# Attention stage: batch loops written out and interleaved, powers of the successor matrix made in the first loop

## The reference

```python
Xq = (H @ W_lin.T).reshape(bt, n, h, dh)
Xv = (H @ W_val.T).reshape(bt, n, h, dh)
e = einsum('behd,hd->beh', leaky_relu(Xq[:, src] + Xq[:, dst], 0.2), a) + log(A0[src, dst] + EPS)
m = segment_max(e_t, src)            # per source node, over its edges
ex = exp(e_t - m[src]); attn = ex / segment_sum(ex, src)[src]
Y = segment_sum(attn * Xv[dst], src)
return Y @ W_out.T
```

## Time and profile before

| | us |
|---|---|
| median of 3 runs | 6786.41 (6783.37 to 6788.06) |
| the profiled execution's own time | 6792.14 |
| its span, first to last instruction | 6790.4 |
| TensorE busy | 5355.4 (79%) |
| VectorE busy | 4564.6 (67%) |
| ScalarE busy | 2311.9 (34%) |
| mean granted TensorE clock | 0.93 of full |

### The profile page before, as it was taken

One profiled execution on the slowest core, in us unless ns is written; L12 is line 12 of the kernel. 1 busy time (PEld: TensorE's weight loads), 2 busy tenths in 40 slices (PEclk: granted clock), 3 DMA queues, 4 the chain that ended last, 5 costly groups with the idle time before them and its releaser, 6 DMA issues. The chain is left out here.

```text
span 6790.4 us, 109815 instructions
## 1 busy us (share of the span) xinstructions
PE 5355.4 (79%) x33047; PEld 3803.4 (56%) x33047; DVE 4564.6 (67%) x27007; ACT 2311.9 (34%) x7369; POOL 93.6 (1%) x128
## 2 busy tenths in 40 slices
PE   4666788888877769969899976993546699776999
PEld 4555566666666534446566653662333477554676
DVE  7888888888888853379999997775562333424333
ACT  1222222222222235449599881110110233201333
POOL 0000000000000000000000000000000000000000
PEclk9999999999999999969999987996778799876999
DMA  1000000000000000010000000000000000000000
GB/s 46 2 2 2 2 3 5 3 4 4 4 4 3 4 21 13 7 54 6 6 4 6 4 3 8 1 1 0 25 28 0 13 0 0 9 0 13 0 0 25
DMA packets 27823, 56.57 MB, mean 8 GB/s; under 512 B 6186, under 2 KB 16835, under 8 KB 25539
## 3 DMA queue, kind: packets, MB, share of 16 engines
q1 hardware_dynamic: 27330, 50.79, 2.2%
HBM read 38.20 MB, written 12.58 MB: 7 GB/s over the span
## 5 line engine op out<-in xcount | busy, mean ns | idle before, releaser
L2007 DVE SCALAR_TENSOR_TENSOR f_ACC<-f_yp,f_CG,f_ACC 128x128 f32<-128x128 f32 x1024 | 288.4, 344 | 461.6 <-DVEq L2005 461.6
L1952 PEld LDWEIGHTS f_yp<-f_W,f_hs 128*128 128x128 f32 x4096 | 490.0, 192 | 92.6 <-issue 91.8
L1886 PE MATMUL f_hp<-f_rows,f_W 128*128 128x512 f32 x1024 | 531.5, 602 | 5.1 <-ACT U L1896 3.0
L1054 ACT ACTIVATE e_XD<-e_X,e_scal 128x60 f32<-128x60 f32 x2048 | 527.5, 333 | 17.5 <-DVEq L918 15.7
L710 PE MATMUL h_small<-h_part,ones 128*128 128x2 f32 x1024 | 300.6, 363 | 294.3 <-DVE h_jd L579 198.4
L1983 ACT ACTIVATE f_hs<-f_hp,f_b 128x512 f32<-128x512 f32 x512 | 347.7, 685 | 539.7 <-ACTq L1982 539.7
L655 ACT ACTIVATE h_VW<-h_v,h_s 128x8 f32<-128x8 f32 (+3 forms) x512 | 154.8, 302 | 1082.6 <-DVE h_s L417 1082.6
L1942 PE MATMUL f_hp<-f_XT,f_W 128*128 x1024 | 484.4, 601 | 33.0 <-PEq L2236 33.0
L703 PEld LDWEIGHTS h_ax<-h_XM,h_parts 128*128 128x128 bf16 x11520 | 480.8, 114 | 40.9 <-issue 40.9
L1952 PE MATMUL f_yp<-f_W,f_hs 128*128 128x128 f32 x4096 | 493.5, 275 | 0.0
L710 PEld LDWEIGHTS h_small<-h_part,ones 128*128 128x128 f32 x1024 | 256.6, 311 | 415.0 <-DVE h_jd L579 287.6
(11 more groups left out here) (716 smaller groups left out, 11363.2 us busy)
## 6 DMA issues: line engine op xcount, KB each, us to landing
f_S<-in_f_W SPq DMA_DIRECT2D x64, 128.0 KB, 2.3
X<-in_x SPq DMA_DIRECT2D x1, 4096.0 KB, 16.3
held<-g0e_HL SPq DMA_DIRECT2D x16, 256.0 KB, 2.0
g_HL<-held SPq DMA_DIRECT2D x16, 256.0 KB, 2.8
f_W<-in_f_W SPq DMA_DIRECT2D x2, 2048.0 KB
spill<-f_xts SPq DMA_DIRECT2D x16, 256.0 KB, 2.0
f_rows<-spill SPq DMA_DIRECT2D x16, 256.0 KB, 2.7
f_W<-in_f_W SPq DMA_DIRECT2D x4, 1024.0 KB
```

The lines of the kernel that those rows point to most:

```text
L1054: ins = nc.scalar.activation(XD[b][:, k, h, :], X[:, :], ACT.Identity, bias=scal[b][:, k, 2 * h:2 * h + 1])
L1886: nc.tensor.matmul(self.hp[s % 3][:, :], self.W1[:, e, j * P:(j + 1) * P], self.rows[:, g % 2, :], start=True, stop=True).then_inc(self.h_ ...
L1952: ins = nc.tensor.matmul(yp[:, u % 2, k, :], hs[:, u % 2, c, k * P:(k + 1) * P], W2[:, u * UC + c, :], start=(c == 0), stop=(c == UC - 1))
L2007: ins = V_.scalar_tensor_tensor(ACC[:, k, :], yp[:, u % 2, k, :], CG[:, k * E + e:k * E + e + 1], ACC[:, k, :], ALU.mult, ALU.add)
```

## The change

Both loops are written out (no `Fori`, semaphores count up to 16 and are waited for by their value). TensorE's order in turn t of the first loop becomes: PGa of batch t, PL and PV of batch t - 1, then in turns 1, 3, ..., 13 one squaring of the successor matrix (PN and PNT), then PS of batch t - 2. VectorE normalizes batch t + 1 at the head of turn t. PL, PS and PV have one PSUM bank each instead of two; the freed banks hold PN and PNT. `NT` keeps all eight powers (8 instead of 2 halves), ScalarE copies PN to `NX`, VectorE PNT to `NT`. A max round is then PM and one maximum, written in place to `MM`; `MN` is gone. The last sum has its own PSUM tile. In the second loop TensorE makes PY of batch t, then PO of batch t - 1, and VectorE weights batch g + 2 before it adds batch g. Eleven semaphores are new, three are gone.

The diff, cut to its core:

```diff
-        NX, NT = sb("NX", [P, 2, EB, NE]), sb("NT", [P, 2, EB, NE])
+        NX, NT = sb("NX", [P, 2, EB, NE]), sb("NT", [P, 8, EB, NE])
...
+            def round_at(turn):
+                return turn // 2 if turn % 2 == 1 and turn // 2 < ROUNDS - 1 else None
...
                 def _(dve):
+                    def rows(g):
+                        if g >= 2:
+                            dve.wait_ge(g_made, g - 1)
+                        normalize(nc, dve, ch, done, XG[:, g % 2], X, mean, rstd, g * GT, GT).then_inc(xg_full, 1)
+                    rows(0)
+                    for turn in range(B + 2):
+                        if turn + 1 < B:
+                            rows(turn + 1)
+                        if 1 <= turn <= B:
+                            g = turn - 1
+                            dve.wait_ge(v_made, g + 1)
+                            V_.tensor_copy(VT[:, :, g, :], PV[:, 0:EB * D].rearrange("p (e d) -> p e d", e=EB)).then_inc(vt_full, 1)
+                            dve.wait_ge(lx_full, g + 1)
...
+                            V_.scalar_tensor_tensor(LR[:, g % 2, :], LX[:, g % 2, :], 0.2, LX[:, g % 2, :], ALU.mult, ALU.max).then_inc(l_full, 1)
+                        if round_at(turn) is not None:
+                            r = round_at(turn)
+                            dve.wait_ge(jump_made, r + 1)
+                            V_.tensor_copy(NT[:, r + 1, :, :], PNT[:, :, :]).then_inc(nt_full, 1)
+                        if turn >= 2:
+                            g = turn - 2
+                            dve.wait_ge(s_made, g + 1)
...
                 def _(pe):
-                    with pe.Fori(0, B // 2) as i:
+                    for turn in range(B + 2):
+                        if turn < B:
+                            pe.wait_ge(xg_full, turn + 1)
+                            if turn >= 2:
+                                pe.wait_ge(g_full, turn - 1)
...
+                        if 1 <= turn <= B:
+                            g = turn - 1
+                            pe.wait_ge(g_full, g + 1)
+                            if g >= 1:
+                                pe.wait_ge(lx_full, g)
+                            nc.tensor.matmul(PL[:, 0:NE], linT[:, :], GS[:, g % 2, 0:NE], start=True, stop=True).then_inc(l_made, 1)
+                            if g >= 1:
+                                pe.wait_ge(vt_full, g)
...
+                        if round_at(turn) is not None:
+                            r = round_at(turn)
+                            if r > 0:
+                                pe.wait_ge(nx_full, r)
+                                pe.wait_ge(nt_full, r)
...
+                        if turn >= 2:
+                            g = turn - 2
+                            pe.wait_ge(l_full, g + 1)
+                            if g >= 1:
+                                pe.wait_ge(ee_full, EB * g)
...
                 def _(act):
+                        if round_at(turn) is not None:
+                            r = round_at(turn)
+                            act.wait_ge(jump_made, r + 1)
+                            nc.scalar.copy(NX[:, (r + 1) % 2, :, :], PN[:, :, :]).then_inc(nx_full, 1)
...
                     for r in range(ROUNDS):
+                        pe.wait_ge(max_in, r + 1)
                         for e in range(EB):
                             for f in range(EB):
+                                ins = nc.tensor.matmul(PM[:, e, 0:BH], NT[:, r, f, e * P:(e + 1) * P], MM[:, f, :], start=(f == 0), stop=(f == 1))
+                        ins.then_inc(max_out, 1)
...
                     for r in range(ROUNDS):
-                        V_.tensor_tensor(MN[:, :, :], MM[:, :, :], PM[:, :, :], ALU.max).then_inc(ch, 1)
-                        V_.tensor_copy(MM[:, :, :], MN[:, :, :]).then_inc(ch, 1)
-                            V_.tensor_copy(NX[:, b, :, :], PN[:, :, :]).then_inc(ch, 1)
-                            V_.tensor_copy(NT[:, b, :, :], PNT[:, :, :]).then_inc(ch, 1)
+                        dve.wait_ge(max_out, r + 1)
+                        V_.tensor_tensor(MM[:, :, :], MM[:, :, :], PM[:, :, 0:BH], ALU.max).then_inc(max_in, 1)
...
+                    weighted(0)
+                    weighted(1)
+                    for g in range(B):
+                        if g + 2 < B:
+                            weighted(g + 2)
+                        dve.wait_ge(po_made, g + 1)
+                        xs = X[:, g * GT:(g + 1) * GT, :].rearrange("p a b -> p (a b)")
+                        V_.tensor_tensor(xs, xs, flat(PO[:, g % 2, :, :]), ALU.add).then_inc(x_added, 1)
...
+                    for turn in range(B + 1):
+                        if turn < B:
+                            pe.wait_ge(av_full, turn + 1)
+                            if turn >= 2:
+                                pe.wait_ge(yt_full, turn - 1)
...
+                        if turn >= 1:
+                            g = turn - 1
+                            pe.wait_ge(yt_full, g + 1)
+                            if g >= 2:
+                                pe.wait_ge(x_added, g - 1)
```

More of the change, by code:

```diff
@@ L3343, in _ @@
                     V_ = nc.vector
[L3344 to L3360, removed]
-                            for e in range(EB):
[L3362 to L3366, removed]
@@ L3374, in _ @@
                             for n in range(NB):
-                                ins = nc.tensor.matmul(PGa[:, b, :], XG[:, b, n, :], OC[:, n, :], start=(n == 0), stop=(n == NB - 1))
+                                ins = nc.tensor.matmul(PGa[:, turn % 2, :], XG[:, turn % 2, n, :], OC[:, n, :], start=(n == 0), stop=(n == NB - 1))
                             ins.then_inc(g_made, 1)
[L3377 to L3380, removed]
+                        if 1 <= turn <= B:
[6 more added lines that the diff above has]
+                                pe.wait_ge(vt_full, g)
@@ L3390, in _ @@
+                        if turn >= 2:
[3 more added lines that the diff above has]
+                                pe.wait_ge(ee_full, EB * g)
+                            for e in range(EB):
+                                ins = nc.tensor.matmul(PS[:, e * HD:(e + 1) * HD], LR[:, g % 2, e * P:(e + 1) * P], aa[:, :],
                                                        start=True, stop=True)
@@ L3504, in _ @@
                 def _(pe):
-                    with pe.Fori(0, B // 2) as i:
-                        for b in range(2):
-                            pe.wait_ge(av_full, 1)
-                            pe.sem_inc(av_full, -1)
+                    for turn in range(B + 1):
+                        if turn < B:
+                            pe.wait_ge(av_full, turn + 1)
+                            if turn >= 2:
+                                pe.wait_ge(yt_full, turn - 1)
                             for e in range(EB):
-                                ins = nc.tensor.matmul(PY[:, b, :], AV[:, b, e, :], OST[:, e, :], start=(e == 0), stop=(e == 1))
+                                ins = nc.tensor.matmul(PY[:, turn % 2, :], AV[:, turn % 2, e, :], OST[:, e, :], start=(e == 0), stop=(e == 1))
@@ L3520, in _ @@
                 def _(act):
-                    with act.Fori(0, B // 2) as i:
-                        for b in range(2):
-                            act.wait_ge(yt_made, 1)
-                            act.sem_inc(yt_made, -1)
-                            nc.scalar.copy(YT[:, b, :], PY[:, b, :]).then_inc(yt_full, 1)
+                    for g in range(B):
+                        act.wait_ge(yt_made, g + 1)
+                        if g >= 2:
+                            act.wait_ge(po_made, g - 1)
+                        nc.scalar.copy(YT[:, g % 2, :], PY[:, g % 2, :]).then_inc(yt_full, 1)
 def program(nc, d, out):
```

138 lines of the change are left out of this document (53 added, 85 removed).

## The result

The median fell from 6787.2 to 6692.1 us, a ratio of 0.9859 (95% interval 0.9847 to 0.9871), 95.1 us; forecast were 6691 and 95.4 us. A second comparison of five rounds gave 6786.0 and 6687.6, ratio 0.9855 (0.984 to 0.987), 98.4 us less. The profiled execution took 6687.5 us, its span is 6685.5.

A forecast was written before the change was run, and what follows sets the result against it. TensorE was taken to bound all three attention stretches, with pauses and a lowered clock. Gains of 15.1 + 54.4 + 26.3 - 0.4 = 95.4 us put the median at 6691 us, range 6680 to 6708.

The forecast's parts named there:

- First loop: Attention's first loop: TensorE turns of 4.77 us, 16 times, plus 24.0 us of powers; 104.6 us, 15.1 less.
- the slow start of 1.8: First loop's entry: sixteen PGa records start slowly once, 8.80 us against 7.0, costing 1.8 us.
- the cover of VectorE's work: First loop: VectorE, 2.1 us a turn plus 0.7 every second turn, hides behind TensorE's 4.77; copies cost nothing.
- Max rounds: Rounds between the loops: squarings and copies go, a round takes 2.60 us at the low clock; 24.4 us, 54.4 less.
- the two bounds: Max rounds: a PM group takes 1.96 us at the low clock or 1.1 at the high; the low was taken.
- rival A: Max rounds keep the high clock: PM groups take 1.1 us, 7.8 us less, of which 0.5 is counted; 6684; 17%.
- the tail from the last maximum: End of the max rounds, last maximum to last product: 4.87 us less the copy MN to MM, 4.6.
- Second loop: Attention's second loop: turns of 2.61 us, 16 times, and one slow start of 2.65; 46.1 us, 26.3 less.
- Small terms: Stage end: eight more semaphore clears on SyncE cost 0.4 us; fetching written-out code taken at nothing.
- Fetching: Both written-out loops: fetching code instead of repeating it taken at nothing, with 6 us kept for the range.
- B: Both loops: hand-offs don't hide, TensorE waits 0.43 us in each of 32 turns, 14 us; 6705; 14%.
- C: Both loops: the clock stays low throughout, first loop 203.1 us, second 85.3; slower, 6829; 2%.

The follow-up runs named there:

- e3: The changed kernel without the squaring of the successor matrix and its copies, every round using the first matrix; first loop 80.5 us, rounds 23.2, median 6668.9.
- e10: The changed kernel with every first-loop normalization made twice on VectorE, once into a tile nobody reads; first loop 107.2 us, whole 6690.5 us (one run).
- e5: The changed kernel with MM and PM of the max rounds padded from 64 to 128 columns with zeros; rounds 15.9 us, median 6683.6 us.
- e8: The changed kernel with 47 more one-column memsets on VectorE in the setup, shifting later code; next stage's statistics 16.4 us, whole 6698.2 us (one run).
- e7: The changed kernel with the powers made in the max rounds again, both new loops kept; first loop 80.6 us, rounds 59.5, median 6697.9 us.
- e4: The kernel before with both hardware loops written out in the old order, nothing interleaved; first loop 113.1 us, second 60.5, median 6769.1 us.

## Why the prediction was right

**Shape.** TensorE was what each stretch waited for, and after the change it runs without pauses in both loops. The three terms stand beside what was measured as follows.

**First loop**, forecast 104.6, measured 104.7. The turn (4.77 against 4.76 us), the powers (24.0 against 24.2 by e3), the start (1.25 against 1.16) and the slow start of 1.8 (8.83 us for sixteen records, 8.80 before) all hold, and so does the cover of VectorE's work (e10). ScalarE's was not tried by a run; that TensorE never waits for it in the loop shows that it was covered, but not by how much. What was not seen: 6.6 of the 15 us come without any interleaving, since the loop-back was part of the pause.

**Max rounds**, forecast 24.4, measured 21.7. The choice between the two bounds was right, PM takes 1.97 us from the third round on, for the reason weighed there against rival A: the short products decide, with the pauses as they are (e5); whether they would bring the clock down without any pause was not tried. The term was too large by 2.7 us: a round is 2.42 us and not 2.60, mostly because the hand-off from VectorE is shorter (0.06 us from the maximum's end to PM, where 0.21 had been taken from the kernel before); the tail from the last maximum is 4.29 and not 4.6; and two first groups ran fast, 1.5 us in all instead of 0.5. In three of the six traces with 64-column rounds (e3, e8, e10, 23.2 us each) no group ran fast, so the last part is chance. Three hand-offs can be told apart for the 0.21 us: in the kernel before VectorE waits for its own instruction, raises the semaphore by a separate one, and TensorE clears it; in e7 the clearing is gone and it is 0.12 us, from the end of this copy to PM at 6020.39:

```profile
6019.58 0.69 DVE L3488 COPY g_NT<-g_QT 128x512 f32<-128x512 f32 x1
```

In the changed kernel the instruction raises the semaphore itself, and it is 0.06.

**Second loop**, forecast 46.1, measured 45.0. The turn of 2.61 us is exact. The slow start cost 1.75 (5.35 for eight PY records against 3.6) and not 2.65.

**Small terms.** Closing the stage takes 2.83 us from the last addition to the next stage's first instruction where it took 2.42, the 0.4 of the eight more clears. Fetching was taken at nothing in the loops, and nothing shows there. A loop behind them, which the forecast did not look at, became 1.05 us slower by the place of its code.

**Sum.** The stretches and their borders give 99.8 us, less 1.05, 98.7, against a forecast of 95.4. The borders alone shrank by 0.3 us, where the forecast had them grow by 0.4. The two comparisons of medians gave 95.1 and 98.4. That the first met the forecast within a microsecond is luck of the run; the errors of the terms were 2.7 and 1.1 us, both towards more gain, and lay inside the range. The profiled execution took 6687.5 us where 6696.7 had been forecast; 6.3 of these 9.2 us are the earlier start of the attention, behind code that the change did not touch (5924.0 against 5930.3 us), and are not counted to the change.

**Rivals.** A (the clock stays high in the rounds) did not come, although the rounds' pauses are the shortest of all. By the rule of the Trainium skill that the prediction set beside this rival (TensorE: Matmul & The Clock Gate, section "Why this matters for your kernels") it would have come; the traces decide otherwise, with pauses of 0.45 us and a clock of 0.55. What rival A priced against rounds that are slow throughout, 7.8 us with PD, is near what e5's 15.9 us are below the 23.2 of such rounds, 7.3. B (waits in each turn) did not come: no wait of TensorE ahead of PGa or PY beyond the first. C did not come either, 0.98 and 0.96.

## What to carry to other kernels

When TensorE pauses once a pass, count the slow start behind the pause as well, and before anything is rearranged check how much of the pause is the loop-back: 0.6 to 0.7 us a pass here, and in the second loop the clock fell in four of seven pauses with it and in none without it. A chain of 64-column products with small pauses ran at about half clock here; padding them to 128 columns, and two dense products in a pause where TensorE had nothing to do, gave the clock back at no cost (7 us of 175). Price work that is moved by what the clock does in both places, not by the rows of the slow place alone.

## What the runs showed of the hardware that was not expected

- PM with 64 columns brought the granted clock to 0.55 with pauses of 0.45 us; with 128 columns and the same pauses it was 1.00. Eight records took 1.16 us wide and fast, 1.97 narrow and slow.
- All pauses of 2.50 us in the first loop of before, and of 1.90 to 2.28 us in that of e4, ended in a slow start (8.5 to 10.2 us for sixteen records), the seven of 1.61 us in the second loop of e4 did not. But of the seven of 2.31 to 2.34 us in the second loop of before three left the clock high, and of those of 1.89 us in e7's rounds four did (PM groups of 1.10 and 1.11 us). So the length of a pause alone does not decide.
- The place of a loop's code on VectorE changed its time from 16.4 to 17.5 us, 6%, with the same instructions.
- Code ahead of the attention that no edit touched moved its start by up to 12.6 us from one execution to the next (5917.7 in e3, 5930.3 in before). Of that 7.8 us are there already at e_XD's first use (2983.6 and 2991.4 us), the rest comes later. What varies there was not looked into.
